# Decoder layers: the reciprocals of the softmax sums reach 64 partitions a head through DRAM or through TensorE, and the order in which the sync engine issues

## The chip, the cores and the metric

One Trainium2 chip, one of its cores. The metric is the time of one execution on the device in microseconds (us), taken as the median of the runs. Lower is better. The engines are TensorE (PE; PEld is its weight load), VectorE (DVE), ScalarE (ACT), GpSimd (POOL) and the sync engine (SP), which issues DMAs here. Each engine works through its own instructions in order; they wait for each other by semaphores.

## The reference

Two blocks of layers work on x of shape 2 x 512 x 128. The change touches only the second part of the first block, a decoder of four layers with pre-normalisation, eight heads of 64 columns, and a context of 154 rows. Cut to what matters:

```python
def attn_block(xq, ctx, Wq, Wk, Wv, Wo, bo, pe_q, pe_k, mask):
    q = (xq @ Wq).reshape(b, n, HEADS, DH).transpose(0, 2, 1, 3)
    k = (ctx @ Wk).reshape(b, j, HEADS, DH).transpose(0, 2, 1, 3)
    v = (ctx @ Wv).reshape(b, j, HEADS, DH).transpose(0, 2, 1, 3)
    q = apply_rope(q * DH ** (-0.5), pe_q)
    k = apply_rope(k, pe_k)
    sim = jnp.einsum('bhid,bhjd->bhij', q, k)
    ...
    a = jax.nn.softmax(sim, axis=-1)
    out = jnp.einsum('bhij,bhjd->bhid', a, v)
    out = out.transpose(0, 2, 1, 3).reshape(b, n, INNER)
    return out @ Wo + bo
...
for l in range(DEPTH):
    h = rmsnorm(x, sg[l])
    x = attn_block(h, h, sWq[l], sWk[l], sWv[l], sWo[l], sbo[l], pe_q, pe_q, mask) + x
    h = rmsnorm(x, cg[l])
    x = attn_block(h, chunked_seq, cWq[l], cWk[l], cWv[l], cWo[l], cbo[l], pe_q, pe_k, None) + x
    h = rmsnorm(x, fg[l])
    x = jax.nn.gelu(h @ fW1[l] + fb1[l], approximate=False) @ fW2[l] + fb2[l] + x
```

Before these layers stands a linear attention, behind them a mixture of eight experts, a second attention with decay, a cross-attention with 16 heads and a second mixture of experts. They are the same in both kernels.

## The kernel before

**Units and steps.** A layer's attention is cut into 16 units, numbered 0 to 15 in a layer (`u.n % 16`). Units 0 to 7 are self-attention, 8 to 15 cross-attention. A unit is one batch entry and one pair of heads (`u.b`, `u.j`). A self unit has four steps, one for 128 queries each; a cross unit has two, each of 256 queries. So a layer has 48 steps, 32 and 16, and behind them an end part (END) with the feed-forward and the start of the next layer.

**A step.** TensorE turns (transposes) the exponentials of its own step into banks 4 and 5 (`turn_probs`, L1433 for self, L1430 for cross), computes the scores of the step two further on (`scores`, L1414 and L1407), and weighs the values of an earlier unit with turned exponentials (`weigh`, L1455) into bank 6, which holds both heads of the pair, 64 partitions each. Then come small pieces of other work, as the tables SELF, CROSS and END name them: projections (k, q, ck, cq on L1474), values (v, cv on L1479), turned inputs (turn, L1501), output projections (sout, cout and the feed-forward's down, L1486). VectorE takes the maximum of each row of scores (`top`, L798 or L795) and ropes the projections (L786, L787). ScalarE computes the exponentials and, with them, their row sums into `sums` (L1179, L1175), and copies the turned tiles from banks 4 and 5 to KA (L1191, L1188).

**The reciprocals.** When the last step of a unit has its exponentials, VectorE takes 1/sum of all rows (`reciprocals`, L816): `recs` holds them with the 128 queries of a tile on the partitions. The weighed values in bank 6 have the queries along the free axis. So TensorE spreads each reciprocal (`spread`, L1466): 8 matmuls with the identity, with a reciprocal broadcast to 64 columns as weights, put them into bank 7, each value in 64 partitions and its place in the row. Bank 7 is the bank of the projections too. ScalarE copies it to `recT` (`spread_out`, L1196), which has two buffers, and VectorE multiplies (`normalise`, L822): AT <- bank 6 x recT. That product frees bank 6 for the next unit, and the output projections read AT.

**What sets the order.** The order is written out by hand. WEIGH says in which steps a unit is weighed, SPREAD and DONE follow from it: self unit u (0 to 6) is weighed in steps 4u+4 to 4u+7, spread in 4u+6 and multiplied in 4u+7; unit 7 does all of it in step 32; cross unit 8+c is weighed in 34+2c and 35+2c, spread in 34+2c, multiplied in 35+2c; unit 15 is done in the end part. On VectorE the reciprocals of a unit stand at the start of the step behind its last one: step 4u+4 for self, 34+2c for cross unit 8+c. In a step VectorE's order is: reciprocals, the two maxima, the product, then the pieces.

**The sync engine** issues every load of weights. In the layers it waits for the last reader of a buffer and then issues the next layer's weights, one after another, with no other work.

Of the kernel before, what the change touches and what calls it, by code (L numbers as in the profile page):

```python
# [13 lines left out]
P = 128  # L14
B, S, D = 2, 512, 128
NT = B * S
TB = S // P
# [62 lines left out]
DONE = {u: at[-1] for u, at in WEIGH.items()}  # L80

Unit = namedtuple("Unit", "n l cross b j tiles end")
Step = namedtuple("Step", "unit k g before after weigh spread done pieces dve late")
# [5 lines left out]
class Order:  # L89


    def __init__(self):
# [12 lines left out]
        for l in range(LAYERS):  # L105
            mine = bare[48 * l:48 * l + 48]
            units = {i: next(x.unit for x in mine if x.unit.n % (2 * UNITS) == i) for i in range(2 * UNITS)}
            for s, x in enumerate(mine):
                weigh = [(units[i], k) for i, at in WEIGH.items() for k, t in enumerate(at) if t == s]
                roped = True  # L110
                self.turned.append((self.turned[-1][0] + 1 + roped, self.turned[-1][1] + 1 - roped))
                self.steps.append(x._replace(
                    dve=not roped, late=s in LATE,
                    before=mine[s - 1] if s else None, after=mine[s + 2] if s < 46 else None, weigh=weigh,
                    spread=[units[i] for i, t in SPREAD.items() if t == s],
                    done=[units[i] for i, t in DONE.items() if t == s],
                    pieces=self.pieces((SELF + CROSS)[s], l, None, None, None)))
            self.steps.append(self.alone(END, l, mine[47], bare[48 * l + 48:48 * l + 50]))
# [6 lines left out]
    def pieces(self, text, l, unit, last, first):  # L125
        out = []
        for word in text.split():
# [22 lines left out]
            if what in ("norm", "turn"):  # L150
                j, at = self.stage[b]
            out.append(Piece(what, at, b, j, unit, first[j] if what == "first" else last, bank if what == "up" else bank[0], last or first or what in EARLY))
        return out
# [43 lines left out]
def decoder(nc, a, out):  # L197
    ctx = ExitStack()
    with ctx:
# [41 lines left out]
        tops = sb("tops", [P, 4, 2, 2])  # L241
        sums = sb("sums", [P, 4, TB, 2])
        recs = sb("recs", [P, 4, TB, 2])
        recT = sb("recT", [P, 2, S])
# [92 lines left out]
        class q:  # L337
# [48 lines left out]
            spread_full = sem("spread_full")  # L386
            spread_ready = sem("spread_ready")
            mv_ready = sem("mv_ready")
            root_ready = sem("root_ready")
# [66 lines left out]


        block = ctx.enter_context(nc.Block())


        @block.sync
        def _(sp):
# [57 lines left out]
            load_ff(0)  # L520
            for l in range(LAYERS):
                if l:
                    sp.wait_ge(q.y_ready, made["cout", l - 1, 1, 0])
                    load_cout(l)
                    if l + 1 < LAYERS:
                        sp.wait_ge(q.y_free, biases(l - 1))
                        load_small(l + 1)
                    sp.wait_ge(q.y_ready, made["down", l - 1, 1, 0])
                    load_ff(l)
                if l + 1 < LAYERS:  # L530
                    sp.wait_ge(q.roped, made["q", l, 1, PAIRS - 1])
                    sp.wait_ge(q.v_ready, made["v", l, 1, TB - 1])
                    load_self(l + 1)
                    sp.wait_ge(q.y_ready, made["sout", l, 1, 0])
                    load_sout(l + 1)
                    sp.wait_ge(q.v_ready, made["cv", l, 0, 2 * B - 1])
                    sp.wait_ge(q.roped, made["cq", l, 1, PAIRS - 1])
                    load_cross(l + 1)
                else:
                    sp.wait_ge(q.roped, made["q", l, 1, PAIRS - 1])  # L540
                    sp.wait_ge(q.v_ready, made["v", l, 1, TB - 1])
                    load_expert0(0, 0)
            sp.wait_ge(q.y_ready, made["down", LAYERS - 1, 1, 0])
# [149 lines left out]
        def _(dve):  # L693
# [124 lines left out]
            def normalise(u):  # L818

                dve.wait_ge(q.spread_ready, u.n + 1)  # L820
                dve.wait_ge(q.weighed, u.n + 1)
# [318 lines left out]
        def _(act):  # L1140
# [26 lines left out]
            def exps(step, e):  # L1167
# [4 lines left out]
                if u.cross:  # L1172
                    for t in range(2):
                        w = slice(t * C, (t + 1) * C)
                        ins = c.activation(to[:, w], bank[i][:, w], ACT.Exp, bias=tops[:, g % 4, e, t:t + 1],  # L1175
                                           accum_out=sums[:, n, 2 * k + t, e:e + 1])
                    ins.then_inc(q.probs_ready, 1)
                else:
                    c.activation(to, bank[i][:, :], ACT.Exp, bias=tops[:, g % 4, e, 0:1], scale=-1.0,  # L1179
                                 accum_out=sums[:, n, k, e:e + 1]).then_inc(q.probs_ready, 1)  # L1180

# [12 lines left out]
            def spread_out(u):  # L1194
                act.wait_ge(q.spread_full, u.n + 1)
                c.activation(recT[:, u.n % 2, :], bank[7][:, :], ACT.Copy).then_inc(q.spread_ready, 1)  # L1196
# [155 lines left out]
        def _(pe):  # L1352
# [107 lines left out]
            def spread(u):  # L1460
# [3 lines left out]
                for t in range(TB):  # L1464
                    for e in range(2):
                        ins = mm(bank[7][rows_of(e), t * P:(t + 1) * P], recs[:, u.n % 4, t, e:e + 1].broadcast_to([P, DH]),  # L1466
                                 ident[:, :], start=True, stop=True)
# [448 lines left out]
```

## Time and profile before

| | us |
|---|---|
| median of 3 runs | 1398.38 (1397.79 to 1398.71) |
| profiled execution, its own time | 1397.06 |
| its span | 1395.0 |
| PE busy | 1255.1 (90%) |
| DVE busy | 710.3 (51%) |
| ACT busy | 742.3 (53%) |
| POOL busy | 399.2 (29%) |
| TensorE clock granted, mean | 0.955 of full speed |

The span runs from the first to the last instruction of one profiled execution; its own time is the device time of that execution. Busy times overlap between engines. A line such as L1466 is a line of the kernel before; since most instructions come from helpers, a line stands for a kind of work, not for one place. Layers 0 to 3 lie at about 70, 308, 546 and 785 us and each takes 237 us.

### The profile page before, as it was taken

The numbers are of one execution on the slowest core, as the hardware profiler recorded it, in microseconds if no ns is written. First come the engines' busy times: TensorE is split into PE (matmuls) and PEld (weight loads), VectorE is DVE, ScalarE is ACT, GpSimd is POOL, SyncE is SP. The second block draws the span as 40 slices with busy tenths as digits, with TensorE's granted clock in tenths as the row PEclk, the third lists the DMA queues.
The fourth block names the chain that finished last, engine by engine and source line by source line (L and its number), as shares of the span: only waits on it lengthen the run. The fifth ranks groups of instructions, "written<-read, shape, count | busy, mean of one in ns | idle before, by whom it ended". The sixth has DMA issues, their size and how long they took to land.

```text
span 1395.0 us, 21171 instructions
## 1 busy us (share of the span) xinstructions
PE 1255.1 (90%) x7630; PEld 754.9 (54%) x7630; DVE 710.3 (51%) x2061; ACT 742.3 (53%) x1897; POOL 399.2 (29%) x379
## 2 busy tenths in 40 slices
PE   4499998989999898999989899998759995898898
PEld 2244555554455464445556445465449993454687
DVE  6665554356555435555543555644334115675454
ACT  1176666637666654765664576665323444364332
POOL 1343332254332316324321633422220101110100
PEclk8599999999999999999999999999969998899799
DMA  4000000010000001000000000000011100000010
GB/s 142 0 1 0 24 1 9 23 29 2 0 24 8 2 24 29 1 1 23 9 24 8 16 1 1 16 2 1 1 56 31 38 25 0 1 1 1 9 35 24
DMA packets 27096, 22.49 MB, mean 16 GB/s; under 512 B 4342, under 2 KB 22131, under 8 KB 26995
## 3 DMA queue, kind: packets, MB, share of 16 engines
q1 hardware_dynamic: 26995, 21.14, 5.2%
q8 instruction: 64, 1.05, 0.3%
q14 instruction: 37, 0.30, 0.1%
HBM read 20.60 MB, written 0.52 MB: 15 GB/s over the span
## 4 chain that ended last, share of the span: by engine, by line
PE 83%; DVE 9%; POOL 3%; ACT 2%; issue 1%; DMA 0%; SPq 0%; DVEq 0%; POOLq 0%
PE bank L1455 13%; PE bank L1414 10%; PE bank L1433 8%; PE bank L1474 7%; PE bank L1486 6%; PE bank L1466 4%; PE bank L1631 4%; PE bank L1430 4%; PE bank L1407 3%; PE bank L1479 3%; PE bank L1569 2%; PE bank L1571 2%; PE bank L1570 2%; PE bank L1847 2%; PE bank L1538 1%; PE bank L1735 1%
## 5 line engine op out<-in xcount | busy, mean ns | idle before, releaser
L798 DVE CUSTOM_DVE_ANT_0 bank<-bank,maskrow 128x512 f32<-128x512 f32 x256 | 172.3, 715 | 151.5 <-PE bank L1414 151.3
L1179 ACT ACTIVATE probs<-bank,tops 128x512 f32<-128x512 f32 x256 | 174.3, 685 | 128.0 <-DVE tops L798 127.9
L612 POOL TENSOR_TENSOR rot<-rot,sin 128x512 f32<-128x512 f32 (+1 forms) x112 | 134.3, 1199 | 376.2 <-DVE rot L787 376.2
L1191 ACT ACTIVATE KA<-bank 128x512 f32<-128x512 f32 x256 | 139.1, 600 | 31.8 <-PE bank L1433 31.8
L1414 PE MATMUL bank<-QA 64*128 64x512 f32 x512 | 146.6, 653 | 7.7 <-DVE rot L787 7.0
L1433 PEld LDWEIGHTS bank<-ident,probs 128*128 128x128 f32 x1024 | 116.8, 141 | 54.4 <-issue 45.5
L1433 PE MATMUL bank<-ident,probs 128*128 128x128 f32 x1024 | 134.7, 274 | 2.3 <-ACT Vs L1156 2.3
L1455 PE MATMUL bank<-KA,Vs 128*64 128x512 f32 x512 | 135.4, 615 | 0.0
L1175 ACT ACTIVATE probs<-bank,tops 128x154 f32<-128x154 f32 x256 | 95.5, 383 | 57.1 <-DVE tops L795 56.6
L614 POOL TENSOR_TENSOR QA<-rot 128x512 f32<-128x512 f32 x96 | 121.8, 1269 | 7.5
L786 DVE TENSOR_TENSOR rot<-bank,cos 128x512 f32<-128x512 f32 (+1 forms) x112 | 73.8, 659 | 74.3 <-PE bank L1474 55.6
L795 DVE TENSOR_REDUCE tops<-bank 128x2 f32<-128x308 f32 x128 | 54.8, 469 | 96.5 <-PE bank L1407 96.5
L1466 PEld LDWEIGHTS bank<-ident,recs 128*64 128x64 f32 x1024 | 58.5, 137 | 61.1 <-issue 48.8
L594 POOL TENSOR_TENSOR rstd<-var,neghalf 128x4 f32<-128x4 f32 x24 | 24.4, 1017 | 230.3 <-DVE var L846 230.0
L1466 PE MATMUL bank<-ident,recs 128*64 128x128 f32 x1024 | 68.0, 275 | 20.9 <-DVE rot L787 12.2
L1188 ACT ACTIVATE KA<-bank 128x512 f32<-128x512 f32 (+1 forms) x128 | 67.6, 584 | 26.6 <-PE bank L1430 26.4
L822 DVE TENSOR_TENSOR AT<-bank,recT 128x512 f32<-128x512 f32 x64 | 44.1, 688 | 69.4 <-PE bank L1455 52.5
L965 DVE SCALAR_TENSOR_TENSOR x<-bank,gates,x 128x128 f32<-128x128 f32 x128 | 36.1, 345 | 83.0 <-PE bank L1631 70.6
L787 DVE STREAM_SHUFFLE rot<-bank 128x512 f32<-128x512 f32 (+1 forms) x112 | 77.8, 695 | 0.0
L1455 PEld LDWEIGHTS bank<-KA,Vs 128*64 128x64 f32 x512 | 26.4, 135 | 87.6 <-issue 86.9
L1256 ACT ACTIVATE probs<-bank,wv 128x512 f32<-128x512 f32 x64 | 43.8, 688 | 54.0 <-PE bank L1571 53.9
L1430 PE MATMUL bank<-ident,probs 128*128 128x128 f32 (+1 forms) x512 | 68.6, 277 | 0.0
(250 smaller groups left out, 2191.5 us busy)
## 6 DMA issues: line engine op xcount, KB each, us to landing
f<-in_fW SPq DMA_DIRECT2D x8, 256.0 KB, 3.1
Vc<-in_wup SPq DMA_DIRECT2D x8, 192.0 KB, 2.5
wk<-in_sWk SPq DMA_DIRECT2D x4, 256.0 KB, 2.8
wq<-in_sWq SPq DMA_DIRECT2D x4, 256.0 KB, 3.2
wv<-in_sWv SPq DMA_DIRECT2D x4, 256.0 KB, 4.1
wo<-in_sWo SPq DMA_DIRECT2D x4, 256.0 KB, 3.7
ck<-in_cWk SPq DMA_DIRECT2D x4, 256.0 KB, 2.7
cv<-in_cWv SPq DMA_DIRECT2D x4, 256.0 KB, 3.1
```

Source lines behind the costliest of these rows:

```text
L612: g.tensor_tensor(turned, turned, tab, ALU.mult).then_inc(q.pool_step, 1)
L614: g.tensor_tensor(dst, r[:, 0, 0:w], r[:, 1, 0:w], ALU.add).then_inc(q.rope_ready, 1)
L798: v.tensor_tensor_reduce(bank[i][:, :], bank[i][:, :], maskrow[:, u.b * S:(u.b + 1) * S], -SCALE, 3.0e38, ALU.add, ALU.min, tops[:, g % 4, ...
L1175: ins = c.activation(to[:, w], bank[i][:, w], ACT.Exp, bias=tops[:, g % 4, e, t:t + 1], accum_out=sums[:, n, 2 * k + t, e:e + 1])
L1179: c.activation(to, bank[i][:, :], ACT.Exp, bias=tops[:, g % 4, e, 0:1], scale=-1.0, accum_out=sums[:, n, k, e:e + 1]).then_inc(q.probs_rea ...
L1191: c.activation(turned_self(u)[:, half, :, k * P:(k + 1) * P], bank[4 + half][:, :].rearrange("p (c t) -> p c t", t=P), ACT.Copy).then_inc( ...
L1414: mm(bank[first + e][:, :], QT[rows_of(e), u.j, c0:c0 + P], KT[rows_of(e), u.j, u.b * S:(u.b + 1) * S], start=True, stop=True).then_inc(q. ...
L1430: ins = turn(o, ring[:, r + e, t * C + c0:t * C + c0 + n], ident[:, :])
L1433: ins = turn(bank[4 + half][:, t * P:(t + 1) * P], ring[:, r + half, t * P:(t + 1) * P], ident[:, :])
L1455: ins = mm(bank[6][rows_of(e), :], vals, src, start=(k == 0), stop=(k == u.tiles - 1))
L1466: ins = mm(bank[7][rows_of(e), t * P:(t + 1) * P], recs[:, u.n % 4, t, e:e + 1].broadcast_to([P, DH]), ident[:, :], start=True, stop=True)
L1474: mm(bank[i][:, 0:n], w[:, j * P:(j + 1) * P], rhs, start=True, stop=True).then_inc(q.proj_full, 1)
```

## The change

Of the 16 units of a layer only unit 7 (NEAR) keeps the spreading on TensorE and the copy on ScalarE. For the 15 others the sync engine waits for the reciprocals, stores them to a tensor in DRAM (`dram_r`, four slots) so that the 512 values of a head lie in a row, waits until the store has landed, and loads each head's row to 64 partitions of `recT`. VectorE's product waits for those two loads. `sums` and `recs` have their last two axes exchanged. The sync engine now walks through the steps of the order and issues the weights of later layers at set steps (3, 34, 36, 42), between the units' transfers.

```diff
+NEAR = (7,)
+def rows_sent(n):
+    return sum(i % (2 * UNITS) not in NEAR for i in range(n + 1))
...
-                    spread=[units[i] for i, t in SPREAD.items() if t == s],
+                    spread=[units[i] for i, t in SPREAD.items() if t == s and i in NEAR],
...
+            if what == "spread" and 2 * UNITS - 1 not in NEAR:
+                continue
...
-        sums = sb("sums", [P, 4, TB, 2])
-        recs = sb("recs", [P, 4, TB, 2])
+        sums = sb("sums", [P, 4, 2, TB])
+        recs = sb("recs", [P, 4, 2, TB])
...
+        dram_r = nc.dram_tensor("dram_r", [4, 2, TB, P], F32)
...
+            def send_rows(u):
+                i = u.n % 4
+                sp.wait_ge(q.rec_ready, u.n + 1)
+                sp.dma_start(dram_r[i].rearrange("e t p -> p (e t)"), recs[:, i, :, :].rearrange("p e t -> p (e t)"),
+                             allow_slow_non_contiguous=True).then_inc(q.rec_out, 16)
+                sp.wait_ge(q.rec_out, 16 * rows_sent(u.n))
+                if u.n >= 2:
+                    sp.wait_ge(q.heads_ready, u.n - 1)
+                for e in range(2):
+                    sp.dma_start(recT[e * DH:e * DH + DH, u.n % 2, :],
+                                 dram_r[i, e].rearrange("t p -> (t p)").partition_broadcast(DH)).then_inc(q.spread_in, 16)
+            def loads(l, s):
+                if l and s == 3:
...
+            for step in ORDER.steps:
+                if step.unit:
+                    last = step.before and step.before.unit
+                    if last and step.k == 0 and last.n % (2 * UNITS) not in NEAR:
+                        send_rows(last)
+                    loads(step.unit.l, step.g % 48)
+                for p in step.pieces:
+                    if p.what == "out" and 2 * UNITS - 1 not in NEAR:
+                        send_rows(p.step.unit)
...
-                dve.wait_ge(q.spread_ready, u.n + 1)
+                if u.n % (2 * UNITS) in NEAR:
+                    dve.wait_ge(q.spread_ready, u.n + 1 - rows_sent(u.n))
+                else:
+                    dve.wait_ge(q.spread_in, 32 * rows_sent(u.n))
```

Three places show what the order of the instructions becomes. The line numbers of the kernel after differ from those of before.

TensorE, layer 0, steps 34 and 35 (cross-attention, unit 8: L1407 scores, L1455 weighing, L1466 spreading, L1430 turned exponentials, L1479 values), before:

```order
L1407 MATMUL bank<-KTc,QA 128x154 x3
L1455 MATMUL bank<-KA,Vc 64x512 [waits turned_act,v_ready,heads_ready]
L1455 MATMUL bank<-KA,Vc 64x512
L1466 MATMUL bank<-ident,recs 64x128 [waits y_ready,rec_ready]
L1466 MATMUL bank<-ident,recs 64x128 x7
L1430 MATMUL bank<-ident,probs 128x128 [waits turned_act,probs_ready]
```

and after:

```order
L1449 MATMUL bank<-KTc,QA 128x154 x3
L1497 MATMUL bank<-KA,Vc 64x512 [waits turned_act,v_ready,heads_ready]
L1497 MATMUL bank<-KA,Vc 64x512
L1472 MATMUL bank<-ident,probs 128x128 [waits turned_act,probs_ready]
L1472 MATMUL bank<-ident,probs 128x128 x3
```

The spreading and its wait for the reciprocals are gone between the weighing and the next step's turned exponentials.

VectorE two steps on, units 9 and 10 (L816 reciprocals, L795 maxima, L822 product, L786 and L787 rope), before:

```order
L816 RECIPROCAL recs<-sums 128x8 [waits probs_ready]
L795 TENSOR_REDUCE tops<-bank 128x2 [waits scores_full] x4
L822 TENSOR_TENSOR AT<-bank,recT 128x512 [waits weighed,spread_ready]
L786 TENSOR_TENSOR rot<-bank,cos 128x512 [waits rope_ready,proj_full]
L787 STREAM_SHUFFLE rot<-bank 128x512
L816 RECIPROCAL recs<-sums 128x8 [waits probs_ready]
```

and after:

```order
L855 RECIPROCAL recs<-sums 128x8 [waits probs_ready]
L834 TENSOR_REDUCE tops<-bank 128x2 [waits scores_full] x4
L864 TENSOR_TENSOR AT<-bank,recT 128x512 [waits weighed,spread_in]
L825 TENSOR_TENSOR rot<-bank,cos 128x512 [waits rope_ready,proj_full]
L826 STREAM_SHUFFLE rot<-bank 128x512
L855 RECIPROCAL recs<-sums 128x8 [waits probs_ready]
```

Nothing has moved; the product waits for the loads (spread_in) in place of ScalarE's copy (spread_ready), and the reciprocals of the next unit stand behind it as before.

The sync engine behind the first loads of weights, before:

```order
L498 DMA f<-in_fW 128x4x128
L484 DMA wk<-in_sWk 128x512 [waits v_ready,roped]
L484 DMA wq<-in_sWq 128x512
L484 DMA wv<-in_sWv 128x512
L487 DMA wo<-in_sWo 128x4x128 [waits y_ready]
```

and after:

```order
L513 DMA f<-in_fW 128x4x128
L540 DMA dram_r<-recs 128x8x1 [waits rec_ready]
L546 DMA recT<-dram_r 64x512 [waits rec_out]
L546 DMA recT<-dram_r 64x512
...
L540 DMA dram_r<-recs 128x8x1 [waits rec_ready]
L546 DMA recT<-dram_r 64x512 [waits heads_ready,rec_out]
L546 DMA recT<-dram_r 64x512
L499 DMA wk<-in_sWk 128x512 [waits v_ready,roped]
```

Between the loads of weights now stand a store and two loads for each unit, eight units' worth before the first weights of the next layer.

## Rows read from the trace of the kernel before

**Rows 1.** The page: parts 1 and 4, whole run.

```profile
PE 1255.1 (90%) x7630; PEld 754.9 (54%) x7630; DVE 710.3 (51%) x2061; ACT 742.3 (53%) x1897; POOL 399.2 (29%) x379
...
PE 83%; DVE 9%; POOL 3%; ACT 2%; issue 1%; DMA 0%; SPq 0%; DVEq 0%; POOLq 0%
```

**Rows 2.** Line L1466, PE, whole run; waits: total us, times, longest.

```profile
L1466 PE MATMUL bank<-ident,recs x1024: 272/273/323, 97.8 to 993.7; 128*64 128x128 f32 x171
...
PE bank L1466 <- DVE rot L787: 12.2, 8, 1.5
...
PE bank L1466 <- DVE recs L816: 5.3, 8, 0.7
...
PE bank L1466 <- ACT hT L1147: 3.5, 4, 0.9
```

**Rows 3.** Chain in order of time, layer 1, self-attention: start us, us.

```profile
419.09 0.87 PE bank L1466 x16
419.96 1.02 PE bank L1433 x8
...
424.11 0.87 PE bank L1433 x8
```

**Rows 4.** VectorE in order of time, unit 6: start us, us, idle before.

```profile
425.39 0.19 DVE L816 RECIPROCAL recs<-sums 128x8 f32<-128x8 f32 x1
...
438.12 0.69 DVE L822 TENSOR_TENSOR AT<-bank,recT 128x512 f32<-128x512 f32 x1 [0.23 <-PE bank L1455]
```

**Rows 5.** PE in order of time, layer 1, cross-attention.

```profile
453.55 1.09 PE L1466 MATMUL bank<-ident,recs 128*64 128x128 f32 x16 [0.66 <-DVE recs L816]
...
471.70 1.09 PE L1466 MATMUL bank<-ident,recs 128*64 128x128 f32 x16 [1.52 <-DVE rot L787]
```

**Rows 6.** VectorE in order of time, layer 1, cross-attention.

```profile
453.30 0.20 DVE L816 RECIPROCAL recs<-sums 128x8 f32<-128x8 f32 x1
...
457.52 0.69 DVE L822 TENSOR_TENSOR AT<-bank,recT 128x512 f32<-128x512 f32 x1 [0.23 <-PE bank L1455]
...
467.28 0.69 DVE L786 TENSOR_TENSOR rot<-bank,cos 128x512 f32<-128x512 f32 x1 [1.78 <-PE bank L1474]
...
468.52 0.18 DVE L816 RECIPROCAL recs<-sums 128x8 f32<-128x8 f32 x1
...
497.58 0.69 DVE L832 TENSOR_TENSOR y<-bank,y 128x512 f32<-128x512 f32 x1 [3.00 <-PE bank L1486]
...
500.56 0.20 DVE L816 RECIPROCAL recs<-sums 128x8 f32<-128x8 f32 x1
...
511.99 0.19 DVE L816 RECIPROCAL recs<-sums 128x8 f32<-128x8 f32 x1
517.89 0.69 DVE L822 TENSOR_TENSOR AT<-bank,recT 128x512 f32<-128x512 f32 x1 [5.72 <-PE bank L1455]
```

**Rows 7.** Chain in order of time, end of layer 1.

```profile
517.78 7.36 PE bank L1486 x64
...
525.16 0.70 DVE y L832
```

**Rows 8.** DMA view of 1390.4 to 1392.4 us: packets, MB, share; issue to landing.

```profile
q1 hardware_dynamic: 528, 0.26, 43.7%
...
out_x<-x SPq DMA_DIRECT2D x2, 256.0 KB, 2.3
```

**Rows 9.** DMA view of 528 to 540 us, and an issue on the sync engine.

```profile
lrow<-in_lrow SPq DMA_DIRECT2D x1, 192.0 KB, 2.9
...
163.24 0.33 SPq L484 DMA_DIRECT2D wk<-in_sWk  x1
```

**Rows 10.** DMA view of 1129.5 to 1130.2 us (0.7 us).

```profile
DMA packets 198, 0.03 MB, mean 36 GB/s; under 512 B 153, under 2 KB 198, under 8 KB 198
...
q1 hardware_dynamic: 198, 0.03, 22.4%
```

**Rows 11.** The page, part 3: DMA queue of the whole run.

```profile
q1 hardware_dynamic: 26995, 21.14, 5.2%
```

More of the change, by code:

```diff
@@ L387, in decoder @@
             spread_ready = sem("spread_ready")
+            rec_out = sem("rec_out")
+            spread_in = sem("spread_in")
             mv_ready = sem("mv_ready")
@@ L520, in _ @@
             load_ff(0)
-            for l in range(LAYERS):
-                if l:
+            def send_rows(u):
[11 more added lines that the diff above has]
+                if l and s == 3:
                     sp.wait_ge(q.y_ready, made["cout", l - 1, 1, 0])
@@ L529, in _ @@
                     load_ff(l)
-                if l + 1 < LAYERS:
+                if s == 34:
                     sp.wait_ge(q.roped, made["q", l, 1, PAIRS - 1])
                     sp.wait_ge(q.v_ready, made["v", l, 1, TB - 1])
-                    load_self(l + 1)
+                    if l + 1 < LAYERS:
+                        load_self(l + 1)
+                    else:
+                        load_expert0(0, 0)
+                if l + 1 < LAYERS and s == 36:
                     sp.wait_ge(q.y_ready, made["sout", l, 1, 0])
                     load_sout(l + 1)
+                if l + 1 < LAYERS and s == 42:
                     sp.wait_ge(q.v_ready, made["cv", l, 0, 2 * B - 1])
@@ L538, in _ @@
                     load_cross(l + 1)
[L539 to L542, printed above, removed]
+            for step in ORDER.steps:
[7 more added lines that the diff above has]
+                        send_rows(p.step.unit)
             sp.wait_ge(q.y_ready, made["down", LAYERS - 1, 1, 0])
@@ L818, in normalise @@
             def normalise(u):
-                dve.wait_ge(q.spread_ready, u.n + 1)
+                if u.n % (2 * UNITS) in NEAR:
+                    dve.wait_ge(q.spread_ready, u.n + 1 - rows_sent(u.n))
+                else:
+                    dve.wait_ge(q.spread_in, 32 * rows_sent(u.n))
                 dve.wait_ge(q.weighed, u.n + 1)
@@ L1175, in exps @@
                         ins = c.activation(to[:, w], bank[i][:, w], ACT.Exp, bias=tops[:, g % 4, e, t:t + 1],
-                                           accum_out=sums[:, n, 2 * k + t, e:e + 1])
+                                           accum_out=sums[:, n, e, 2 * k + t:2 * k + t + 1])
                     ins.then_inc(q.probs_ready, 1)
@@ L1179, in exps @@
                     c.activation(to, bank[i][:, :], ACT.Exp, bias=tops[:, g % 4, e, 0:1], scale=-1.0,
-                                 accum_out=sums[:, n, k, e:e + 1]).then_inc(q.probs_ready, 1)
+                                 accum_out=sums[:, n, e, k:k + 1]).then_inc(q.probs_ready, 1)
             def turned_out(step, half):
@@ L1194, in spread_out @@
             def spread_out(u):
-                act.wait_ge(q.spread_full, u.n + 1)
+                act.wait_ge(q.spread_full, u.n + 1 - rows_sent(u.n))
                 c.activation(recT[:, u.n % 2, :], bank[7][:, :], ACT.Copy).then_inc(q.spread_ready, 1)
@@ L1465, in spread @@
                     for e in range(2):
-                        ins = mm(bank[7][rows_of(e), t * P:(t + 1) * P], recs[:, u.n % 4, t, e:e + 1].broadcast_to([P, DH]),
+                        ins = mm(bank[7][rows_of(e), t * P:(t + 1) * P], recs[:, u.n % 4, e, t:t + 1].broadcast_to([P, DH]),
                                  ident[:, :], start=True, stop=True)
```

## The prediction, made before the changed kernel had run

> **What bounds the kernel now.** The reader starts with the page: TensorE (PE) is busy 90% of a span of 1395.0 us, and the chain of work that ended last lies on PE for 83% [rows 1]. So work that leaves PE shortens the run, as far as nothing else is just behind it. Next comes the line to be removed, L1466, the spreading of the reciprocals: 1024 passes, that is 64 units of 8 matmuls at two passes each. The view of the waits says how long PE's matmuls stood still before them: 5.3 us for the reciprocals (8 times), 12.2 us for a rope (8 times, since bank 7 is shared with the projections), 3.5 us for an input (4 times) [rows 2]. Then the chain in order of time, in a self-attention stretch: it runs through each spread, 0.87 us, and the transposes behind a spread take 1.02 us where all others take 0.87 [rows 3]. A spread thus costs PE 0.87 + 0.15 = 1.02 us. The four layers repeat each other every 237 us, so I work out layer 1 (about 310 to 550 us) and multiply by four.
>
> **Removed.** 15 of 16 spreads in each layer, 60 in all; unit 7 of each layer keeps its own. In self-attention (units 0 to 6) that is 7 x 1.02 = 7.1 us a layer, all on the chain. In cross-attention (units 8 to 15) it is 8 x 1.02 = 8.2 us, and with it go PE's waits: 21.0 / 4 = 5.2 us a layer [rows 2]. More than 13.4 us can't be had there. ScalarE loses 60 copies of a bank to recT; it isn't on the chain there and I count nothing.
>
> **Added.** For each of the 60 units the row of reciprocals goes recs, then DRAM, then recT, and VectorE's product (L822) waits for that instead of for ScalarE's copy. Call L the time from the end of the reciprocals to recT being there. L is a serial sum, since the sync engine waits for the store to land before it issues the loads:
> - Sync engine sees the reciprocals, issues: 0.05 us.
> - Store S, 1024 words of 4 B that don't lie together, 64 on each of 16 DMA engines. The only store in the trace, a half of the output, lands 2.3 us after its issue; in 2.0 us its 528 packets of 512 B keep the 16 engines 43.7% busy, so a packet takes 2.0 x 16 x 0.437 / 528 = 26 ns and 33 of them on one engine 0.9 us [rows 8]. The rest, 1.4 us, is fixed. No row shows a store of single words. From below: in a stretch where 153 of 198 packets are loads or signals under 512 B, a packet takes 0.7 x 16 x 0.224 / 198 = 13 ns [rows 10], so S = 1.4 + 64 x 0.013 = 2.2. From above: the mean packet of the run takes 0.052 x 16 x 1395 / 26995 = 43 ns [rows 11], so S = 4.15. As slow as the stored 512 B packet it would be 3.1. I take 2.7, between the small packets and the stored ones.
> - Sync engine sees the landing, 0.05. Two loads, each one row of 2 KB to 64 partitions; the second is issued some 0.35 us behind the first (one issue takes 0.33), and the nearest row, a row sent to 128 partitions (192 KB), lands after 2.9 us, 3.1 in another layer [rows 9]: 3.4 in all. VectorE sees it: 0.1.
> So L = S + 3.6: 6.3 us as taken, 5.8 from below, 7.75 from above.
>
> The Trainium skill, "DMA: Bandwidth & Descriptors", Anatomy of one DMA, gives a fixed cost of about 2.0 us and bytes over 436 GB/s; by that S would be 2.0 and the pair of loads some 3.0, and the time that of the fast rival below. The store's row agrees with less than that fixed part, 1.4 us. The same page, Rules for kernel authors, speaks against the change: a last dimension that isn't contiguous becomes one descriptor per element and should be rearranged; Specifications adds that below 512 B a DMA reads, modifies and writes. It gives no price for a word. That is the slow rival; no row here can show it.
>
> **Self-attention: L is hidden.** Between a unit's reciprocals and its product lie three steps: from 425.39 to 438.12, 12.7 us, for unit 6, where the room is least [rows 4]; one spread less leaves 11.7, against 6.3. What waits behind the product on VectorE (the rope, later maxima) waits no longer than now. Cost 0. PE is the chain here, VectorE and ScalarE are behind it, so the 7.1 us a layer should come whole.
>
> **Cross-attention: L is exposed.** Here only one step lies between. The product follows the reciprocals by 4.0 us (453.5 to 457.5) for unit 8 and by 5.7 for unit 15 [rows 6], less than 6.3, and part of that goes with the spread; only beside projections and ropes is there more room. And VectorE works in order: the product of a unit stands ahead of the next unit's reciprocals. So the waits don't overlap, they form a new chain: reciprocals of 8, L, product, reciprocals of 9, L, and so on to unit 15. PE waits on it where bank 6 is to be used again (weighing needs the product before) and at the output projection. Sum of this chain in layer 1, from the reciprocals of unit 8, ready at 453.5: eight times L, eight products of 0.69, seven reciprocals at 0.1 net, two ropes that stand between product and reciprocals (1.24 each, 467.28 to 468.52), one residual with its statistics (2.98, 497.58 to 500.56) [rows 6]. That is 8 L + 11.7, so unit 15's product ends at 465.2 + 8 L. Now it ends at 517.89 + 0.69 = 518.6. Behind it comes the last output projection, of two on PE from 517.78 to 525.14, and then, on the chain, VectorE, GpSimd and the next layer's start [rows 7]. The projection takes half of the 7.36, 3.7. It would end at 468.9 + 8 L: gain 56.2 - 8 L a layer. For L = 6.3 that is 5.8; since PE and the stages in between hold the chain up here and there I take off 0.5: **5.3 us a layer**. It is far from the 13.4 that PE gives up: the wait removed on PE comes back on the sync queue. What it is paid with are the small waits of before, 0.66 us at 453.55 and 1.52 at 471.70 [rows 5], and the work of the spreads.
>
> **The sync engine's new order.** Weight loads are now issued at steps 3, 34, 36 and 42, each behind the store and loads of a unit. What they wait for is done by then, except the last rope of step 41, which ends before unit 13's row is ready. What they load is used only from the layer's end part on, more than five steps later. They are issued behind a unit's loads, so they share the DMA engines with those at most. Cost 0; a 256 KB load beside a round trip would lengthen one L a layer by under 1 us.
>
> **Sum.** (7.1 + 5.3) x 4 = 49.6 us. The profiled execution took 1397.06 us (1395.0 and 2.1 around it), so it would take 1347.5; the median of the runs shown is 1.3 above, 1348.8. I say **1349**.
>
> **Rivals.**
> - Fast store (S = 2.2, L = 5.8): 56.2 - 46.4 = 9.8; near the corner at which PE's 13.4 takes over both limits act, so 2 off, 7.8. (7.1 + 7.8) x 4 = 60: 1338 us. For it: small packets take little here. Chance 0.22.
> - The self-attention gain doesn't come, because maxima, exponentials and transposes already run at their own period: 4 x 5.3 = 21, 1377 us. Against it: the chain there is PE without gaps [rows 3]. Chance 0.05.
> - Dear words (S about 4.15, L = 7.75): 56.2 - 62 - 0.5 + 7.1 = 0.8, times 4 is 3: 1395 us, no change to speak of. Chance 0.08.
> - **Slower than before**: words cost more than 43 ns each. The chain of eight round trips turns the balance at 56.2 - 8 L - 0.5 + 7.1 = 0, L = 7.85, S = 4.25, 44 ns a word. At 60 ns S is 5.2, L 8.8: -14.7 + 7.1 = -7.6 a layer, 1429 us. For it: all eight units of a layer wait, and each 1 us of L is worth 32 us of the run. Against: nothing in the trace takes that long for so few bytes. Chance 0.20.
> - My forecast, S from 2.4 to 3.3: 1342 to 1373 with 1349 likeliest. Chance 0.45.
>
> **Chances and range.** Faster by over 0.2% (what a measurement of this kernel can tell from no change): 0.45 + 0.22 + 0.05 and part of the dear words, 0.75. Within 0.2%: 0.05. Slower: 0.20. The range has to reach past the upper bound of S into the slow rival: 1335 to 1408.
>
> **What would show it.** L1466 with 64 passes, PE busy near 1190 us. The store's time from issue to landing: 2.7, and 3 to 3.4 for the loads. VectorE's product waiting on the DMA in cross-attention, about 2 to 3 us each, and never in self-attention (units 0 to 6). From unit 8's reciprocals to unit 15's product 62 us in a layer, now 65. PE waiting for the product before it weighs. Layers 225 us apart instead of 237. I am wrong if the store lands in over 4 us, if products of self-attention wait, or if reciprocals and products turn out not to be in series.

## The result, and the profile of the kernel after

The kernel after takes 1656.74 us (median of 4 runs, 1653.99 to 1661.3), the kernel before beside it 1398.09: a ratio of 1.185, 95% interval 1.182 to 1.189. It is 18.5% slower; the forecast was 1349, the upper end of the range 1408. Its profiled execution has a span of 1651.9 us, 256.9 more than before.

Parts 1, 2 and 4 of the page of the kernel after (busy us; tenths of the clock in 40 slices; shares of the chain that ended last, by engine and by line), to be held against [rows 1]:

```profile
PE 1286.3 (78%) x6670; PEld 742.4 (45%) x6670; DVE 706.5 (43%) x2061; ACT 713.8 (43%) x1837; POOL 399.6 (24%) x379
...
PEclk8699987779998877999978689998777799789799
...
DMA 44%; PE 34%; DVE 11%; issue 5%; POOL 3%; SPq 2%; ACT 2%; DVEq 0%; POOLq 0%
DMA dram_r<-recs 32%; DMA recT<-dram_r 12%; PE bank L1528 5%; PE bank L1673 3%; PE bank L1497 3%; PE bank L1456 2%; PE bank L1611 2%; PE bank L1613 2%; PE bank L1612 2%; PE bank L1889 2%; PE bank L1475 1%; DVE rot L826 1%; SPq L546 1%; DVE rot L825 1%; PE bank L1777 1%
```

The chain lay on PE for 83% and lies on PE for 34% now; a third of it is the store of the reciprocals. PE executes 960 passes fewer and is busy 31 us more. The views of the waits of the kernel after, VectorE and PE and then the sync engine (total us, times, longest):

```profile
DVE AT L864 <- DMA recT<-dram_r: 411.2, 58, 15.2
...
PE bank L1497 <- DVE AT L864: 222.9, 42, 12.1
...
SPq L546 <- DMA dram_r<-recs: 571.7, 57, 11.7
```

The prediction named 2 to 3 us for VectorE's wait in cross-attention, none in self-attention, and 2.7 us for the store. The store was waited for 571.7 / 57 = 10.0 us on average. Such a wait begins when the issue is over, 0.37 us after its start, so counted from the issue, as the prediction counts S, it is about 10.4. One unit of layer 0, the sync engine in order of time (start us, us):

```profile
281.33 0.37 SPq L540 DMA_DIRECT2D dram_r<-recs  x1
292.12 1.09 SPq L546 DMA_DIRECT2D recT<-dram_r  x2
```

and VectorE:

```profile
281.11 0.19 DVE L855 RECIPROCAL recs<-sums 128x8 f32<-128x8 f32 x1
...
296.04 0.69 DVE L864 TENSOR_TENSOR AT<-bank,recT 128x512 f32<-128x512 f32 x1 [9.98 <-DMA recT<-dram_r]
```

From the store's issue to the loads' issue 10.8 us; from the end of the reciprocals (281.30) to the product 14.7, the L of the prediction, which put it at 6.3. And this is not the store's packets. The DMA view of 281.3 to 284.0, 2.7 us from its issue on (packets, MB, share of 16 engines):

```profile
DMA packets 1041, 0.01 MB, mean 5 GB/s; under 512 B 1040, under 2 KB 1040, under 8 KB 1040
...
q1 hardware_dynamic: 1040, 0.00, 17.4%
```

The 1040 packets are the 1024 words and 16 more (a store of 128 pieces has 144, in store_whole below). All of them lie in this stretch, the last some 1.5 us after the issue, at 2.7 x 16 x 0.174 / 1040 = 7 ns each, faster than the 13 ns that the prediction took as its lower bound. The same view of 284 to 292:

```profile
DMA packets 1, 0.02 MB, mean 2 GB/s; under 512 B 0, under 2 KB 0, under 8 KB 0
```

The one packet left is a piece of instructions. So for 8 us the profile shows nothing of the store, and only then is the sync engine told that it has landed.

**The whole slowdown by stage.** The table reads the times of VectorE's reciprocals and products in four layers: from unit 0's reciprocals to unit 8's (self-attention), from there to unit 15's product (cross-attention), from there to the next layer (three of them), and the mean of the 32 cross units from the end of the reciprocals to the product. Each is a mean over layers, in us:

| kernel | self | cross | rest | reciprocals to product |
|---|---|---|---|---|
| before | 128.7 | 64.6 | 45.2 | 6.0 |
| after | 128.6 | 128.9 | 45.3 | 14.7 |
| cross_rows | 128.7 | 124.4 | 45.1 | 14.1 |
| self_rows | 126.3 | 64.6 | 44.7 | 6.0 |
| half_words | 123.9 | 122.3 | 44.9 | 13.9 |
| words_beside | 122.6 | 106.7 | 44.5 | 11.9 |
| words_apart | 122.6 | 66.2 | 42.3 | 6.5 |
| words_by32 | 122.6 | 64.4 | 42.8 | 6.5 |
| words_sbuf | 122.6 | 63.9 | 44.3 | 6.4 |
| store_whole | 122.6 | 62.2 | 45.2 | 5.9 |
| vt_all | 122.6 | 64.6 | 44.1 | 6.5 |
| vt_some | 122.6 | 60.7 | 45.8 | 5.5 |
| vt_self | 122.6 | 64.6 | 45.2 | 6.0 |

Before to after: 4 x (128.9 - 64.6) = 257 us, all of the 256.9, in cross-attention. The prediction's chain (8 L + 11.7 from the reciprocals' end to the product's end, so 8 L + 11.2 in this table's terms) gives 8 x 14.7 + 11.2 = 128.8. The chain was right, the number put into it was not. For short gaps the chain is a lower bound only: before, it gives 8 x 6.0 + 11.2 = 59.2 for the 64.6 measured, since VectorE there also waits for PE between a product and the next reciprocals (1.78 and 3.00 us in [rows 6]). The experiments ask why the store took so long, and then what a short one is worth.

### The profile page after: what moved, and what is told of

The parts are those of the page before. It is cut to its first block, busy times and chain, and to the rows that moved or that the text cites. A ratio compares the mean times of both kernels' runs of the same rounds, so it can differ in the third digit from the quotient of the medians.

```text
span 1651.9 us, 19369 instructions
## 1 busy us (share of the span) xinstructions
PE 1286.3 (78%) x6670; PEld 742.4 (45%) x6670; DVE 706.5 (43%) x2061; ACT 713.8 (43%) x1837; POOL 399.6 (24%) x379
## 4 chain that ended last, share of the span: by engine, by line
DMA 44%; PE 34%; DVE 11%; issue 5%; POOL 3%; SPq 2%; ACT 2%; DVEq 0%; POOLq 0%
DMA dram_r<-recs 32%; DMA recT<-dram_r 12%; PE bank L1528 5%; PE bank L1673 3%; PE bank L1497 3%; PE bank L1456 2%; PE bank L1611 2%; PE bank L1613 2%; PE bank L1612 2%; PE bank L1889 2%; PE bank L1475 1%; DVE rot L826 1%; SPq L546 1%; DVE rot L825 1%; PE bank L1777 1%
## 5 line engine op out<-in xcount | busy, mean ns | idle before, releaser
L1497 PE MATMUL bank<-KA,Vc 128*64 128x512 f32 (+1 forms) x256 | 98.4, 859 | 205.3 <-DVE AT L864 205.3
L864 DVE TENSOR_TENSOR AT<-bank,recT 128x512 f32<-128x512 f32 x64 | 44.3, 692 | 427.5 <-DMA recT<-dram_r 411.2
L1497 PEld LDWEIGHTS bank<-KA,Vc 128*64 128x64 f32 (+1 forms) x256 | 15.9, 171 | 227.9 <-DVE AT L864 215.2
L1472 PEld LDWEIGHTS bank<-ident,probs 128*128 128x128 f32 (+1 forms) x512 | 63.6, 141 | 50.7 <-issue 31.2
L1472 PE MATMUL bank<-ident,probs 128*128 128x128 f32 (+1 forms) x512 | 85.4, 322 | 0.3 <-ACT KA L1230 0.3
L834 DVE TENSOR_REDUCE tops<-bank 128x2 f32<-128x308 f32 x128 | 54.0, 464 | 51.4 <-PE bank L1449 51.2
L1497 PEld LDWEIGHTS bank<-KA,Vs 128*64 128x64 f32 x512 | 26.8, 136 | 107.5 <-issue 76.2
```

Source lines behind the costliest of these rows:

```text
L1472: ins = turn(o, ring[:, r + e, t * C + c0:t * C + c0 + n], ident[:, :])
L1497: ins = mm(bank[6][rows_of(e), :], vals, src, start=(k == 0), stop=(k == u.tiles - 1))
```

## Experiments: the sync engine, and which units pay

**walk_only.** All 16 units keep TensorE's spreading; what is left of the change is the sync engine's walk and the exchanged axes.

```diff
-NEAR = (7,)
+NEAR = tuple(range(16))
```

> All 16 units of a layer keep TensorE's spreading; what is left of the change is the sync engine's walk through the steps, with the later issue of weights, and the exchanged axes of sums and recs. Theory (the walk costs nothing): 1398 us, within 0.2%. Rival (weights that are issued late cost part of the 258 us): over 1405 us.

Measured: 1398.87 us (10 runs) against 1397.97, ratio 1.0003, 0.9994 to 1.0013. The walk and its loads at steps 3, 34, 36 and 42 cost nothing, as the prediction said.

**cross_rows** and **self_rows.** Only cross-attention, or only self-attention, goes over DRAM, with the slow store in both.

```diff
-NEAR = (7,)
+NEAR = tuple(range(8))      # cross_rows
+NEAR = tuple(range(7, 16))  # self_rows
```

> Only the cross-attention units 8 to 15 go through DRAM. Theory (eight round trips in series in each layer, 56.2 minus 8 times 14.7 is a loss of 61 us a layer): 1640 us, within 25. Rival (loss is spread over both halves): under 1560 us.

> Only the self-attention units 0 to 6 go through DRAM, units 7 to 15 keep the spreading. A round trip takes 14.7 us in the kernel after, and the room there is 11.7 to 14.7. Theory (a self unit pays 0 to 3 us of wait, which eats the 1.0 us gained): about 1400 us, between 1385 and 1420. Rival (the room hides it, all of the loss comes from cross-attention): 1370 us.

Measured: cross_rows 1632.3 us (2 runs), ratio 1.167 (1.165 to 1.170); self_rows 1388.89 (4 runs), ratio 0.993 (0.991 to 0.995). The loss is cross-attention's. In self-attention the change is a gain even so, but a third of what was worked out: 9 us instead of 28. The waits of self_rows:

```profile
DVE AT L864 <- DMA recT<-dram_r: 38.3, 19, 3.7
...
SPq L546 <- DMA dram_r<-recs: 265.2, 28, 11.0
```

The room is 11.7 us where it is least; a round trip of about 14 is longer than that, and 19 of the 28 products wait. In the kernel after the self waits (0.3 to 3.7 us each in layer 0) eat the gain altogether. The two halves don't add up: 234 - 9 = 225 us, and the kernel after loses 259. With both over DRAM cross-attention takes 128.9 instead of 124.4 us and self-attention 128.6 instead of 126.3, and the store is waited for 10.0 us instead of 9.5 (293.3 / 31 in cross_rows, 265.2 / 28 in self_rows). Why it is slower with both is open.

## Experiments: what makes the store slow

Theory at the start: single words are dear, by their number (the prediction's term). Rivals: any store takes that long; or it is how the words lie at their destination.

**store_whole.** The same 4 KB, a partition's eight values as one piece of 32 B: 128 pieces instead of 1024. The loads are as before and bring the values in another order, so this kernel leaves out their right place in recT; it is there for its time alone.

```diff
-sp.dma_start(dram_r[i].rearrange("e t p -> p (e t)"), recs[:, i, :, :].rearrange("p e t -> p (e t)"),
-             allow_slow_non_contiguous=True).then_inc(q.rec_out, 16)
+sp.dma_start(dram_r[i].rearrange("e t p -> (e t p)").rearrange("(p c) -> p c", p=P),
+             recs[:, i, :, :].rearrange("p e t -> p (e t)")).then_inc(q.rec_out, 16)
```

> The store writes each partition's 8 reciprocals as one piece of 32 bytes (128 pieces, together one row of DRAM) in place of 1024 single words; the loads are as before, so recT holds the values in a wrong order and the output isn't the reference's. Same bytes, same two DMAs in series. Theory (the single words make the landing late, 10.8 us): the store lands in 2.0 to 2.7 us, L is about 6, and the sum of the prediction holds: 1349 us, within 12. Rival (any store that is waited for by the sync engine takes about 10 us): 1657 us.

Measured: 1355.77 us (4 runs), ratio 0.969 (0.967 to 0.970). The sync engine in order of time:

```profile
259.35 0.33 SPq L540 DMA_DIRECT2D dram_r<-recs  x1
260.77 1.08 SPq L546 DMA_DIRECT2D recT<-dram_r  x2
```

and its waits:

```profile
SPq L546 <- DMA dram_r<-recs: 76.4, 60, 3.0
```

76.4 / 60 = 1.3 us. Same bytes, same slots in DRAM, same load behind it: not stores as such, and not the load of what has just been written. With this one edit the time is within 7 us of the forecast, and that is luck in part. The store lands 1.4 us after its issue and the loads 2.9, and from the reciprocals' end to the rows being there it is 4.8 us where nothing else holds them up (253.72 to 258.50), not 6.3. For L = 4.8 the prediction's 56.2 - 8 L is more than the 13.4 that PE gives up, and its sum would come to at most (7.1 + 13.4) x 4 = 82 us, some 1316 us for the run. The store was faster than forecast, and cross-attention gave less than its L promised.

**half_words.** 512 words, the first head's; the second head's rows in DRAM are filled once at the start with numbers of an input.

```diff
-sp.dma_start(dram_r[i].rearrange("e t p -> p (e t)"), recs[:, i, :, :].rearrange("p e t -> p (e t)"),
+sp.dma_start(dram_r[i, 0].rearrange("t p -> p t"), recs[:, i, 0, :],
```

> The store sends only the first head's 512 words instead of 1024, 32 on each DMA engine; the row in DRAM is filled once at the start with numbers of an input, so the loads bring wrong values for the second head. Store_whole fixed the rest of the path: 1.4 us when no single words are sent, 9 to 10.3 us more with 1024. Theory (every word costs its engine some 140 ns): the store takes about 6 us, L about 10, the run about 1475 us. Rival (a fixed penalty for a store with single words): 10 us and 1657 us as in the kernel after.

Measured: 1607.21 us (one run); the store is waited for 520.0 / 60 = 8.7 us. Half the words save 1.3 of 10.0 us, so the time is far from going with their number.

**words_apart** and **words_sbuf.** Again all 1024 words, each at the start of a 64-byte piece of DRAM of its own (dram_w), or into SBUF. The loads read rows that were filled once at the start.

```diff
+dram_w = nc.dram_tensor("dram_w", [4, 2 * TB, P, 16], F32)
...
+sp.dma_start(dram_w[i, :, :, 0].rearrange("c p -> p c"), recs[...]   # words_apart
+sp.dma_start(wordS[:, i, :, 0], recs[...]                            # words_sbuf
```

> 1024 single words as in the kernel after, but each goes to 64 bytes of its own in DRAM, so no two share a piece of 64 bytes; the loads read a row filled at the start, so their values are wrong. Theory (every word written to DRAM costs, wherever it goes): store about 10 us, 1657 us. Rival (words from different engines that fall into the same 64 bytes hinder each other; in the kernel after 16 neighbours of a row do): store 1.5 to 3 us, 1356 us.

> 1024 single words, 64 on each engine, but sent to SBUF (8 words 8 bytes apart in each of 128 partitions) and not to DRAM; the loads read a row of DRAM filled at the start, so their values are wrong. Theory (it is the writing of a word to DRAM that is slow): the transfer takes 1.5 to 2.2 us, the run 1356 us. Rival (a DMA engine is slow with single words whatever the target): about 10 us and 1657 us.

Measured: 1370.83 and 1366.2 us (one run each). The waits of the sync engine, words_apart:

```profile
SPq L548 <- DMA dram_w<-recs: 143.4, 60, 3.5
```

and the DMA view of one of its stores (2.8 us from the issue on; the store's issue and landing in the last line):

```profile
q1 hardware_dynamic: 1040, 0.00, 16.7%
...
dram_w<-recs SPq DMA_DIRECT2D x1, 4.0 KB, 2.6
```

143.4 / 60 = 2.4 us instead of 10.0, for the same number of packets that take the same 7 ns (2.8 x 16 x 0.167 / 1040). In SBUF it is 107.5 / 60 = 1.8 us. So it is neither the count nor the 4 B alone, but where the words fall in DRAM.

**words_beside.** In the store of the kernel after, neighbouring words of a row come from neighbouring partitions. Here a partition's eight words lie beside each other, still sent one by one. (Which DMA engine moves which partition no run shows, so this can't be told as a matter of engines.)

```diff
+recs = sb("recs", [P, 4, 2, TB, 2])
...
+sp.dma_start(dram_r[i].rearrange("e t p -> (e t p)").rearrange("(p c) -> p c", p=P),
+             recs[:, i, :, :, 0].rearrange("p e t -> p (e t)"),
```

> 1024 single words, but the 8 words of a partition go side by side in DRAM, so that one engine writes whole runs of 32 bytes word by word (recs has its words 8 bytes apart, which keeps the pieces at 4 bytes); recT then holds the values in a wrong order. Theory (every word costs): store about 10 us, 1657 us. Rival (different engines in the same 64 bytes): store 1.5 to 4 us, 1356 to 1380 us.

Measured: 1535.24 us (one run); 443.7 / 60 = 7.4 us for the store. Eight words of one partition that fill one 32-byte piece are slow when sent as eight words, and take 1.3 us as one piece. That different partitions write side by side adds 2.6 us, but isn't needed.

**words_by32.** As words_apart, with 32 B between the words.

```diff
-dram_w = nc.dram_tensor("dram_w", [4, 2 * TB, P, 16], F32)
+dram_w = nc.dram_tensor("dram_w", [4, 2 * TB, P, 8], F32)
```

> The 1024 words are stored one by one, each at the start of a 32-byte piece of DRAM of its own (64 bytes in the run before, where the sync engine waited 2.4 us); the loads read rows filled once at the start, so the values are not the reciprocals. If words are slow that fall into the same 64 bytes, two share a piece here and the wait is clearly over 2.4 us, 3 to 4; the time 1385 to 1410. If the piece that counts is 32 bytes or less, 2.4 us and 1371 as before. If words are slow by the number that share a piece, then 16 (9.5 us), 2 (here) and 1 (2.4 us) lie about on a line: 2.4 + (9.5 - 2.4)/15 = 2.9 us, about 1377.

Measured: 1364.31 us (one run). The sync engine's wait:

```profile
SPq L548 <- DMA dram_w<-recs: 148.8, 60, 3.6
```

148.8 / 60 = 2.5 us, the same as at 64 B. My theory that two words in one 64-byte piece hinder each other falls. What stands: words 4 B apart 7.4 to 10.0 us, 32 B apart or more 2.4 to 2.5. Distances between were not run, and by which mechanism the memory or the DMA engines serve neighbouring words late is open. The traces show only that the packets are over long before: in one store of half_words by 1.3 us after the issue, with the landing at 8.7, in one of words_beside by some 1.9, with the landing at 6.6.

## Experiments: a store of whole pieces that the loads can use

The rows are needed with the queries lying together, the reciprocals stand with them on the partitions. VectorE can turn them in blocks of 32 x 32 before the store, for one small operation. Then a partition's 32 values are queries that lie together: 128 pieces of 128 B, and loads that read 512 B pieces. The product reads bank 6 and recT through views in four dimensions, which put each value where it belongs.

```diff
+recX = sb("recX", [P, 4, 32])
+dram_r = nc.dram_tensor("dram_r", [4, P, 32], F32)
...
+ins = v.transpose(recX[:, n % 4, :], recs[:, n % 4, :])
...
+sp.dma_start(dram_r[i], recX[:, i, :]).then_inc(q.rec_out, 16)
...
+sp.dma_start(recT[e * DH:e * DH + DH, u.n % 2, :].rearrange("p (b x) -> p b x", b=4),
+             dram_r[i].rearrange("(b j) c -> b (j c)", b=4)[:, e * P:e * P + P].partition_broadcast(DH)).then_inc(q.spread_in, 16)
...
+NEAR = (7,)                         # vt_all
+NEAR = (7, 8, 9, 12, 13, 14, 15)    # vt_some
+NEAR = tuple(range(7, 16))          # vt_self
```

> The repair: behind the reciprocals VectorE turns the 128 x 8 values in blocks of 32 x 32 (one more small operation, about 0.2 us), so that the store of each of the 15 units is 128 pieces of 128 B that lie together, and the loads read 512 B pieces. It computes what the reference asks. Theory (what is slow is single words written to DRAM next to each other): the store is waited for 1.3 to 1.6 us as in the run that stores 32-byte pieces, the loads land in 3.3 to 3.6, L is 5.2 to 5.5 with the turning: 1350 to 1365, near that run's 1356. Rival (the loads of 512 B pieces, 4 times as many, or the product read through a turned view, take longer): products over 0.75 us or loads over 4 us, 1370 to 1400. If a store of any kind behind a dependent load took long here, 1500 or more.

> As the repair, but in each layer units 10 and 11 and 7 (before: 7) go over DRAM or not as follows: 0 to 6, 10 and 11, which lie beside projections and ropes, go over DRAM; 7, 8, 9 and 12 to 15 keep TensorE's spreading. If the round trips in series are what limits cross-attention even at L near 5.4, this is as fast as or faster than all 15: 1355 to 1368, made of 4 x 7.1 in self-attention and up to 2 x 1.0 a layer for units 10 and 11. If the chain of round trips has room at L near 5.4 (56.2 - 8 x 5.4 = 13 a layer), it stays behind the one with all 15 by 10 to 30 us.

> As the repair, but only units 0 to 6 of each layer go over DRAM. With the slow store this same choice of units gave 1389, 9 us under the kernel before, of 28 worked out. With L of about 5.4 against 11.7 us of room no product of self-attention should wait for its loads, and the whole 4 x 7.1 = 28 us should come: 1370. If it stays near 1389, it wasn't the wait for the rows that took two thirds of that gain, but something else in self-attention.

| kernel | us (4 runs each) | ratio to before, 95% |
|---|---|---|
| vt_all | 1366.24 | 0.978 (0.975 to 0.980) |
| vt_some | 1356.89 | 0.971 (0.969 to 0.973) |
| vt_self | 1371.65 | 0.982 (0.980 to 0.983) |

The turning in vt_all, VectorE in order of time:

```profile
254.59 0.20 DVE L855 RECIPROCAL recs<-sums 128x8 f32<-128x8 f32 x1
254.82 0.21 DVE L858 STREAM_TRANSPOSE recX<-recs 128x32 f32<-128x32 f32 x1
...
260.62 0.69 DVE L873 TENSOR_TENSOR AT<-bank,recT 128x512 f32<-128x512 f32 x1 [3.99 <-DMA recT<-dram_r]
```

and its DMA issues (KB, us to landing):

```profile
recT<-dram_r SPq DMA_DIRECT2D x120, 128.0 KB, 3.4
dram_r<-recX SPq DMA_DIRECT2D x60, 16.0 KB, 1.4
```

vt_self gains 26 us: without the slow store self-attention gives what the prediction promised (28). vt_some is the fastest of the three, 41 us under before: units 10 and 11, next to the projections, bring 14.8 us over vt_self, 3.7 a layer. There the spread cost PE its 1.09 us and also waits, since bank 7 is shared with the projections [rows 5]: from unit 8's reciprocals to unit 15's product it is 60.7 us instead of 64.6. Taking units 8, 9 and 12 to 15 over DRAM too (vt_all) loses 9.3 us again, though the round trip is 5.8 us where nothing else holds the product up (254.79 to 260.62). vt_all ends 1 us above the range that was expected of it; neither rival is the reason, since the product through the turned view takes 0.69 us as before and the loads 3.4.

**Where that goes.** The prediction's chain gives for a gap of 6.5 us 8 x 6.5 + 11.2 = 63.2, measured is 64.6. So at that gap the round trips alone leave at most 1.4 of a gain, and not even that comes. What becomes of the work that PE was spared, PE in order of time in vt_all shows (start us, us):

```profile
210.35 1.07 PE L1506 MATMUL bank<-KA,Vc 26*64 26x512 f32 x4
...
212.32 1.04 PE L1481 MATMUL bank<-ident,probs 128*128 128x128 f32 x8
...
217.09 1.92 PE L1506 MATMUL bank<-KA,Vc 128*64 128x512 f32 x4 [3.02 <-DVE AT L873]
218.95 1.88 PE L1481 MATMUL bank<-ident,probs 128*128 128x128 f32 x8
```

Behind a wait of 3.02 us the same eight turns take 1.88 us instead of 1.04, and the four weighing matmuls 1.92 instead of 1.07: the lower of the clock's two levels, 1.2 instead of 2.4 GHz. The Trainium skill, "TensorE: Matmul & The Clock Gate", Part 1, says that an idle TensorE is put to half its clock and a busy one back to the full; the trace agrees, 1.88 us behind the wait and 1.04 ahead of it. The windows view, cross-attention of layer 0 (from:to, us, then busy us and count of PE, PEld, DVE, ACT, POOL, then granted clock, DMA share, GB/s), before:

```profile
215.00:281.00 66.00, 59.88 (x450) 34.64 (x447) 25.49 (x71) 42.13 (x139) 16.77 (x14) 1.00 0.05 16
```

vt_all:

```profile
209.00:274.00 65.00, 57.41 (x327) 30.71 (x326) 25.59 (x75) 38.32 (x131) 16.80 (x14) 0.89 0.22 64
```

Eight spreads of 1.09 us less should leave 59.9 - 8.7 = 51.2 us of PE; it is 57.4. So some 6 us of work come back through the clock, and PE is idle for 7.6 us instead of 6.1. In vt_some the clock of this stretch is 0.97. How long the stage would be with PE at the full clock no run shows.

The end of cross-attention in layer 0 of vt_all, where unit 15's product on VectorE ends at 274.57 (L1537: the feed-forward's 32 passes, then the output projection's 32):

```profile
272.19 3.84 PE L1537 MATMUL bank<-f,G 128*128 128x128 f32 x32
275.87 3.74 PE L1537 MATMUL bank<-co,AT 128*128 128x128 f32 x32
```

The projection ends 5.0 us behind the product. The prediction had 3.7, as if it began at once, but PE is still at the passes ahead of it.

The windows view of the kernel after, self-attention and cross-attention of layer 0:

```profile
77.00:205.00 128.00, 120.86 (x604) 56.83 (x602) 75.18 (x212) 82.92 (x207) 49.04 (x42) 1.00 0.08 16
217.00:345.00 128.00, 74.32 (x341) 39.57 (x338) 23.92 (x66) 38.78 (x131) 16.79 (x14) 0.74 0.14 32
```

In cross-attention the clock is 0.74 and PE is busy 74 of 128 us with work of some 51. That explains why PE's busy time rose; it doesn't set the time there, since eight round trips make up the whole stage.

## Why the prediction was wrong, point by point

- **The step that failed is the store, S.** "From above: the mean packet of the run takes ... 43 ns [rows 11], so S = 4.15", and "I take 2.7". Measured: 10.0 us of wait on average, up to 11.7, and about 10.4 from the issue. Both bounds priced the packets and held the fixed part at the 1.4 us of a store of 512 B packets [rows 8]. The packets came in below even the lower bound (7 ns); the time from their end to the signal, which I had called fixed, was 10.8 - 1.5 = 9.3 us in the unit shown. The rest of L, taken as 3.6, was 14.7 - 10.8 = 3.9. An upper bound on a part that isn't the costly one bounds nothing.
- **The slow rival** was the right one in direction, at 0.20, and its turning point (S = 4.25, L = 7.85) nearly stands: by the measured stages it is (64.6 + 6.1 - 11.2) / 8 = 7.4 us. Its mechanism was wrong ("words cost more than 43 ns each": half_words, words_apart), and at 60 ns a word it stopped at 1429. The measured 10.0 us would have been (10.0 - 1.4) / 64 = 134 ns a word, for which I had no row.
- **The rule of the Trainium skill** was weighed and given too little. "DMA: Bandwidth & Descriptors", Rules for kernel authors, says that a last dimension in pieces becomes one descriptor per element and should be rearranged; store_whole against the kernel after is that advice, at 301 us. Its fixed cost of about 2.0 us (Anatomy of one DMA), which the page gives for DMAs that GpSimd issues and the prediction took over for the sync engine without saying so, is over the 1.3 us measured for whole pieces, near the 2.4 us of spread words and far under the 10.0 of neighbouring ones. The same section also says that most of the fixed part is the wait for the memory's receipt of the write, longest when the target is HBM: by that rule the packets could be over long before the signal, and the trace agrees (packets over some 1.5 us after the issue, signal after 10.8).
- **The chain of eight round trips in cross-attention held** where they are long: 8 L + 11.2 gives 128.8 for the 128.9 measured, 122.4 for 122.3 in half_words, 106.4 for 106.7 in words_beside.
- **Self-attention, 7.1 us a layer, held for a short store**: vt_self 26 us of 28; the stage went from 128.7 to 122.6, 6.1, that is 7 x 0.87. The 0.15 us for slower transposes behind a spread don't show there. "Cost 0" for the wait was right for L = 6.3 and wrong for L = 14.7 against 11.7 of room.
- **Cross-attention, 5.3 us a layer, was too much even for a short store.** It was made of 53.4 - 8 L = 3.0 up to unit 15's product, 2.8 behind it for a projection that ends 3.7 us after the product, and 0.5 off. By the columns cross and rest, store_whole gave 2.4 and 0, vt_all 0 and 1.1. For vt_all's own L of 5.8 the formula promised 56.2 - 46.4 - 0.5 = 9.3. Three things were missing. The mean gap is longer than the shortest round trip, 6.5 us. The chain is a lower bound, and 0.5 was taken off where 1.4 (vt_all) to over 3 us (store_whole) had to be; in store_whole the last two products of layer 0 wait for PE, 6.69 and 6.29 us, not for the rows. And the projection isn't alone on PE. PE's half clock behind its new waits, which I had not counted, stands behind part of this, some 6 us of PE's time in layer 0 of vt_all; how much of the stage it costs is argued, not measured.
- **The sync engine's new order, cost 0**: held for the walk (walk_only), not quite beside a round trip, where "under 1 us" on one L a layer was allowed. In vt_all unit 12's gap is 7.2, 7.0 and 6.9 us in the three layers in which weight loads are issued right behind its rows, and 5.7 in the last, which has none.
- **The sum**, put together again with what was measured: 7.1 a layer becomes 0.1, 5.3 becomes -64.3; 4 x -64.2 = -257 us.

## What to carry to other kernels

Before a small store is put into a chain of waits, ask how its pieces lie at the destination, and lay them out as whole pieces (turn them on VectorE first, 0.2 us), since a store's landing isn't the sum of its packets. Count the round trips that are in series, and how much each microsecond of one is worth (here 32 us of the run), before a term without a row gets a narrow bound. And take work off TensorE where it has no wait to put in its place: in vt_all a gap of 3.02 us cost the gap and then 1.7 us more at half the clock (1.92 + 1.88 instead of 1.07 + 1.04).

## What the runs showed of the hardware that I had not expected

- A store of 4 KB in 1024 words of 4 B to DRAM: waited for 7.4 to 10.0 us on average where the words lie 4 B apart, 2.4 to 2.5 at 32 or 64 B, 1.8 into SBUF, 1.3 as 128 pieces of 32 B. Its packets take 7 ns each with the words near (the kernel after) and far (words_apart).
- A broadcast load of two rows of 2 KB to 64 partitions each lands 2.8 to 3.4 us after its issue (medians), in pieces of 2 KB (2.8 in words_apart, 2.9 in store_whole, 3.3 in the kernel after) or of 512 B (3.4 in vt_all); only in half_words was it 4.3, and why is open.
- VectorE's turning of 128 x 32 values in blocks of 32 takes 0.21 us, and its product through a view in four dimensions 0.69 us, as without it.
